# Eight weight buffers and a fourth routed group: moving work across the first table in a macaron MoE–Mamba–MoE kernel

## What is computed

```python
x = x + 0.5 * ffn(layernorm(x), router_w, w1, w2)
x = x + mamba(layernorm(x), ...)
x = x + 0.5 * ffn(layernorm(x), router_w, w1, w2)

def ffn(x, router_w, w1, w2):           # 8 experts, hidden 512, top 2
    logits = einsum('btd,ed->bte', x, router_w)
    top_vals, top_idx = top_k(logits, 2)
    top_w = softmax(top_vals)
    h = square(relu(einsum('nd,edh->enh', x, w1)))
    y = einsum('enh,ehd->end', h, w2)
    return sum over the two chosen experts of top_w * y
```

## Time and profile before

| | |
|---|---|
| median of 3 runs | 1265.07 us (1264.38 to 1267.99) |
| profiled execution | 1260.68 us, its span 1258.9 us |
| mean granted PE clock | 0.931 |
| busy in the span | PE 977.2, DVE 917.3, ACT 743.5, POOL 553.7 us |
| DMA | 154.25 MB moved, mean 123 GB/s |

### The profile page before, as it was taken

The page is one execution under the profiler, slowest core; times in us unless marked ns, Lnnn a source line. Parts: engine busy times, 40 slices in busy tenths (PEclk is TensorE's granted clock), DMA queues, the critical chain, the costliest instruction groups (busy, mean ns, idle before and its releaser), DMA issues.

```text
span 1258.9 us, 41805 instructions
## 1 busy us (share of the span) xinstructions
PE 977.2 (78%) x14928; PEld 824.7 (66%) x14928; DVE 917.3 (73%) x2840; ACT 743.5 (59%) x1751; POOL 553.7 (44%) x611
## 2 busy tenths in 40 slices
PE   1115887999938899999989999998632878899891
PEld 1115776999926677777767677776422767798791
DVE  5676665555528999999989999998866656456765
ACT  3333443566627888888878888887431543465460
POOL 5453455333332345444444444443276454433331
PEclk9998999999968999999999999999755898899996
DMA  9674444454434566666666665654324544445757
GB/s 248 211 224 102 103 108 119 103 103 96 102 101 80 108 112 119 120 116 119 120 117 119 117 119 115 123 108 89 65 77 123 103 104 107 112 110 140 181 125 234
DMA packets 205962, 154.25 MB, mean 123 GB/s; under 512 B 122752, under 2 KB 172928, under 8 KB 205632
## 3 DMA queue, kind: packets, MB, share of 16 engines
q0 software_dynamic: 41952, 72.86, 27.7%
q1 hardware_dynamic: 156896, 72.39, 24.3%
q10 hardware_dynamic: 6912, 6.32, 1.8%
HBM read 41.37 MB, written 56.10 MB: 77 GB/s over the span
## 4 chain that ended last, share of the span: by engine, by line
PE 35%; DVE 31%; issue 12%; DMA 8%; SPq 5%; ACT 4%; another core or an unknown queue 3%; POOL 2%; ACTq 1%; DVEq 0%; POOLq 0%
PE bank L773 15%; PE bank L786 13%; DVE lake L1046 7%; DVE arena L1107 3%; SPq L706 2%; DMA arena<-in_w 2%; DVE q_ L1025 2%; PE bank L1436 2%; DVE lake L1052 2%; ACT lake L1316 2%; DVE lake L1086 1%; DVE lake L1074 1%; DMA X<-yg 1%; DMA lake<-turned_y 1%
## 5 line engine op out<-in xcount | busy, mean ns | idle before, releaser
L773 PE MATMUL bank<-arena,weights 128*128 128x128 f16 x3744 | 256.1, 226 | 37.7 <-issue 30.2
L724 POOL DMA_INDIRECT ychosen<-arena,didx x156 | 157.7, 1011 | 267.5 <-issue 128.0
L773 PEld LDWEIGHTS bank<-arena,weights 128*128 x3744 | 233.7, 101 | 51.0 <-issue 47.3
L786 PE MATMUL bank<-weights,arena 128*128 x1872 | 240.9, 279 | 13.0 <-issue 9.1
L877 DVE TENSOR_TENSOR arena<-arena 128x512 f32<-128x512 f32 x156 | 107.9, 692 | 180.8 <-ACT arena L821 146.8
L821 ACT ACTIVATE arena<-bank 128x512 f32<-128x512 f32 x156 | 93.1, 597 | 212.8 <-PE bank L773 80.0
L786 PEld LDWEIGHTS bank<-weights,arena 128*128 128x128 f16 x1872 | 180.3, 100 | 39.9 <-issue 18.6
L663 POOL DMA_INDIRECT disp<-lake,sloti x128 | 132.7, 1037 | 70.2 <-issue 35.4
L1046 DVE SCALAR_TENSOR_TENSOR lake<-lake,vec 128x128 f32<-128x128 f32 x480 | 128.7, 346 | 0.0
L882 DVE TENSOR_TENSOR arena<-arena 128x512 f16<-128x512 f32 x156 | 108.1, 693 | 5.3
L1192 POOL DMA_DIRECT2D lake<-turned_y x32 | 27.9, 871 | 189.5 <-DMA turned_y<-lake 189.5
(11 more groups left out here) (176 smaller groups left out, 2010.8 us busy)
## 6 DMA issues: line engine op xcount, KB each, us to landing
arena<-in_w SPq DMA_DIRECT2D x16, 512.0 KB
yg<-ychosen SPq DMA_DIRECT2D x32, 256.0 KB, 2.8
X<-yg POOLq DMA_DIRECT2D x64, 128.0 KB, 3.6
arena<-lake SPq DMA_DIRECT2D x128, 64.0 KB, 3.3
lake<-lake POOLq DMA_DIRECT2D x32, 256.0 KB, 4.1
turned_y<-lake SPq DMA_DIRECT2D x128, 64.0 KB, 1.8
lake<-turned_y POOLq DMA_DIRECT2D x32, 256.0 KB, 4.0
lake<-ychosen SPq DMA_DIRECT2D x32, 256.0 KB, 3.7
```

Of the source, the lines that this page charges most:

```text
L724: pool.indirect_dma_start(ychosen, bass.IndirectOffsetOnAxis(ap=didx[:, t % NIDX:t % NIDX + 1], axis=0), ysb[n % YB][:, :], None).then_inc ...
L773: mm = pe.matmul(o, chunk(where, 2 * ("hl".index(w) * WN + c * HID + m * P), P), v, start=c == 0 and n_ == 0, stop=c == KD - 1 and n_ == 2)
L786: mm = pe.matmul(down_ps(n), x, chunk(where, 2 * ((2 + "hl".index(w)) * WN + c * D), D), start=c == 0 and n_ == 0, stop=c == KH - 1 and n_ ...
```

## The change

The staging ring gets eight buffers, and lies at the start of the arena, over the tiles' own buffers (`xTh`, `tails`, `hr`, `hq`, `hh`, `hl`, `ysb`). So SP's first tile load of the kernel waits for 22 used parts (the buffers under `xTh` and `tails`), and the first relu for all 32. With eight buffers the second half of x is queued after the eighth chunk, that is after all of w1. After each of the groups 0 to 3 only 4 parts (w1) are split; the 16 parts of w2 are split behind the first table. Group 4 is no longer routed before the tiles but among them; the statistics of groups 6 and 7 come right behind the first table, in one stretch, in both FFN layers. POOL sends 32 times in the tiles of a layer's first half by a new table, instead of 8 times ahead of the first store and 24 times after. The pads of the second half are all issued by ACT, one behind each of eight tiles. The spare rows of the second half are written after the first four groups. In the second FFN layer the loads and additions of finished rows and their stores begin later. The many step counters of DVE (`Chain`) become one; the waits are the same in number and place.

```diff
-NSTAGE = 3
+NSTAGE = 8
+XTH_FREE = 2 * (NSTAGE + 3)
...
-        used[0] = stage_at
+        used[0] = 0
         stage = [carve(1024) for p in range(NSTAGE)]
...
# route_dve
-                if g + 2 < NG:
+                if g + 2 < HG + 2:
                     stats(g + 2)
...
-                    for k in range(g * 8, g * 8 + 8):
+                    for k in range(g * 4, g * 4 + 4):
                         split_low(dve, k)
                 if g % HG == HG - 1:
                     yield from table(g // HG)
+                if g == HG - 1:
+                    for late in range(HG + 2, NG):
+                        stats(late)
+                    if r == 0:
+                        for k in range(2 * NCHUNK, 4 * NCHUNK):
+                            split_low(dve, k)
+                    yield ("split",)
...
# route_act
-                    for k in range(g * 8, g * 8 + 4):
+                    for k in range(g * 4, g * 4 + 2):
                         split_high(act, k)
                 if g + 1 < NG:
                     turned_rows(g + 1)
                 if r == 0 and g < HG:
-                    for k in range(g * 8 + 4, g * 8 + 8):
+                    for k in range(g * 4 + 2, g * 4 + 4):
+                        split_high(act, k)
+                if r == 0 and g == HG - 1:
+                    for k in range(2 * NCHUNK, 4 * NCHUNK):
                         split_high(act, k)
...
# route_pool
                 spare(0)
-                spare(1)
...
+                if g == HG:
+                    for late in range(HG + 2, NG):
+                        power_of(late)
+                    if r == 0:
+                        spare(1)
...
-        LATE = 14
+        LATE = 18
...
# experts_sync
                 if t == 0:
-                    pads(sp, q, range(0, E, 2))
+                    if p == 0:
+                        pads(sp, q, range(0, E, 2))
...
+                    if n == 0:
+                        sp.wait_ge(S("stage_used"), XTH_FREE)
...
-        POOL_AT = {t: ("sent", 5 + (t - 3) // (2 * GT_), (t - 3) % (2 * GT_)) for t in range(3, 3 + 3 * 2 * GT_)}
+        SEND_AT = {HG: 5, HG + 1: 11, HG + 2: 17, HG + 3: 23}
+        POOL_AT = {at + i * 7 // 8: ("sent", g, i) for g, at in SEND_AT.items() for i in range(2 * GT_)}
...
-        PE_AT = {0: ("turned", 5), 2: ("logits", 5), 5: ("ranks", 5), 6: ("turned", 6), 8: ("logits", 6), 12: ("ranks", 6),
-                 13: ("turned", 7), 15: ("logits", 7), 19: ("ranks", 7)}
+        PE_AT = {3: ("ranks", 4), 4: ("turned", 5), 6: ("logits", 5), 9: ("ranks", 5), 10: ("turned", 6), 12: ("logits", 6),
+                 15: ("ranks", 6), 16: ("turned", 7), 18: ("logits", 7), 21: ("ranks", 7)}
...
-                    pe.wait_ge(S("stage_used"), 4 * NCHUNK)
+                    pe.wait_ge(S("stage_used"), 2 * NCHUNK)
...
-        ACT_AT = {0: ("turned", 5), 2: ("rows", 6), 4: ("ratio", 5), 6: ("turned", 6), 9: ("rows", 7), 11: ("ratio", 6),
-                  13: ("turned", 7), 18: ("ratio", 7)}
-        PADS_AT = 24
+        ACT_AT = {1: ("rows", 5), 2: ("ratio", 4), 5: ("turned", 5), 7: ("rows", 6), 8: ("ratio", 5), 11: ("turned", 6),
+                  13: ("rows", 7), 14: ("ratio", 6), 17: ("turned", 7), 20: ("ratio", 7)}
+        PADS_AT = 25
...
# relu
+                if n == 0:
+                    act.wait_ge(S("stage_used"), 4 * NCHUNK)
...
-                if s == PADS_AT:
-                    pads(act, 2 * r + 1, range(1, E, 2))
-                if r and s >= TILES + LATE + 8 and (s - TILES - LATE - 8) % 5 == 0 and (s - TILES - LATE - 8) // 5 < 4:
-                    store_rows(act, (s - TILES - LATE - 8) // 5)
+                if PADS_AT <= s < PADS_AT + E:
+                    pads(act, 2 * r + 1, [s - PADS_AT])
+                late = s - TILES - LATE - 5
+                if r and 0 <= late < HT and late % 4 == 0:
+                    store_rows(act, late // 4)
...
-        DVE_AT = {0: ("stats", 7), 1: ("norm", 6), 3: ("choose", 5), 4: ("low", 6), 5: ("place", 5), 8: ("norm", 7),
-                  10: ("choose", 6), 11: ("low", 7), 12: ("place", 6), 17: ("choose", 7), 19: ("place", 7),
-                  20: ("table", 1, 0), 21: ("table", 1, 1), 22: ("table", 1, 2), 23: None}
+        DVE_AT = {0: ("norm", 5), 1: ("choose", 4), 2: ("low", 5), 4: ("place", 4), 6: ("norm", 6), 7: ("choose", 5),
+                  8: ("low", 6), 10: ("place", 5), 12: ("norm", 7), 13: ("choose", 6), 14: ("low", 7), 16: ("place", 6),
+                  19: ("choose", 7), 22: ("place", 7), 23: ("table", 1, 0), 24: ("table", 1, 1), 25: ("table", 1, 2), 26: None}
...
-            until(routing, ("place", HG))
+            until(routing, ("split",))
...
-                if r and TILES + LATE - 4 <= s < TILES + LATE - 4 + HT:
-                    combine(dve, s - (TILES + LATE - 4))
+                if r and TILES + LATE - 2 <= s < TILES + LATE - 2 + HT:
+                    combine(dve, s - (TILES + LATE - 2))
```

150 lines of the change are left out of this document (60 added, 90 removed).

## The result

The changed kernel takes 1254.13 us (median of 5 runs, 1250.32 to 1259.26), the kernel before 1265.07 on the same chip: a ratio of 0.990 (95% interval 0.9876 to 0.9924). It is faster by 10.9 us, not by the forecast 31.4, and 1254 lies outside the range of 1221 to 1250. The profiled execution took 1259.26 us (span 1257.5).

The account below looks back on a forecast made before the run. Bounds: SP's ring waiting for DVE's splits before 103 us, sends beside first-half tiles, then PE's own pace. Gains 24.9 (start) + 0 (group 4) + 5 + 1.5 (last half) = 31.4 from 1265.1 give 1234 us, range 1221 to 1250.

Parts of the forecast that it names:

- The start: Start of the first FFN layer: first relu at 80.8 instead of 105.7 us, 24.9 us gained.
- the group pace: Routing before the tiles: DVE takes 11.2 us a group, POOL's 11.9 sets the pace; group 3's sends begin at 60.1.
- the pads: Before the first tile load: four pads take 4.5 us of issue, the load begins 4.3 later, at about 73.
- just fit: DMA budget before the first tile load: 17.2 MB, moved by 62 us at 239, then 297 GB/s.
- the lock between DVE and POOL: Splits beside group sends: by the skill's rule the start gains 17.5 instead of 24.9; judged much less, as rival 0.05.
- Group 4 among the tiles: First-half tiles of both layers: moving group 4's routing there costs 0, range -8 to +8 us for each layer.
- Rival D: First-half tiles: first tiles run free of sends, later ones absorb them; -8 us in each layer, 1218 us; chance 0.12.
- what holds PE: First-half tiles: 32 sends beside them cost PE 1.26 us each, 40.4 us lost, and stay 32 after the change.
- The second layer's start: Second FFN layer's first matmul: it follows the last send's landing, not group 4, so moving that group brings 0.
- The last half: Last half's tiles: later loads and additions gain 5 us (0 to 9.8), the earlier last store of rows 1.5.
- under 8: Last half, a sign that the prediction is right: DVE's waits for block loads stay under 8 us.
- rival A: Start worth less: first groups at 13 us each and DMA late, start gains 9, 1249.6 us; chance 0.13.

Follow-up runs that it names:

- ring3: Changed kernel with three staging buffers, eight splits after each group and none behind the table: ratio 0.9954 to the kernel before, first relu at 105.0 us.
- mamba_late_third: Changed kernel with SP's loads of the Mamba weights moved behind its first eight tile loads: median 1170.73 us, first relu at 84.3 us.
- after_third: The changed kernel, unchanged, run again on the faster kind of chip: median 1170.15 us, first relu at 89.0 us.
- extra_sends: Changed kernel with group 5's eight sends repeated in each layer into a tensor nobody reads: 20.0 us more than the changed kernel, on the chip of 1264 us.
- before_third: The kernel before, unchanged, run again on the faster kind of chip: 1192.86 us, first relu at 105.3 us.
- set 1: One of five sets of runs, each on one chip; the kernel before takes 1195.57 us in it.
- g4_ahead: Changed kernel with group 4 routed ahead of the tiles again, and the tables, early sends and pads of the kernel before: ratio 0.9806 to the kernel before.
- late14: Changed kernel with the second layer's block loads, additions and stores of finished rows back at their earlier places: ratio 0.9804 to the kernel before.
- set 2: One of five sets of runs, each on one chip; the kernel before takes 1263.39 us in it.
- set 4: One of five sets of runs, each on one chip; the kernel before takes 1192.86 us in it.
- mamba_late_again: Changed kernel with the Mamba weights loaded behind the first eight tile loads, in another set: 0.28% faster than with one send a tile, first relu at 84.8 us.

## Why the prediction was wrong, step by step

**The start: right mechanism, term mis-sized, 15 instead of 24.9.** DVE no longer waits behind the ring, and all of the gain comes from it (`ring3`). The working of the group pace fits a chip of 1195 us: sends of group 3 begin at 58.41 (forecast 60.1), and the splits end at 80.4 in `mamba_late_third` (forecast 79.1). The step that failed is the pads: "SP issues the loads of the Mamba weights, then its pads", charged with 4.5 us of issue and 4.3 to the load. The loads themselves were left out twice. Their issue stands ahead of the pads, and their bytes (three of 512 KB, and 128, 82.5 and 64 KB, 1.8 MB together) are missing from the 17.2 MB that "just fit". The 4.5 and the 4.3 come from a kernel that had the same six loads ahead of its pads, but there 3.0 us lay between them (the last load ended at 87.16, the pads began at 90.18); now it is 1.1 us (69.12 and 70.25). A second thing was put at nothing without a reason: the seven spare stores of the second half, 0.9 MB that the change moves to this place. The budget has only the seven of the first half. The profile after, SP, ACT and POOL from 62 to 90 us:

```profile
62.45 1.13 POOL L656 DMA_INDIRECT disp<-lake,sloti  x1 [2.03 <-DVE sloti L410]
63.88 1.45 POOL L656 DMA_INDIRECT disp<-lake,sloti  x1 [0.30 <-issue]
65.64 0.97 POOL L656 DMA_INDIRECT disp<-lake,sloti  x1 [0.30 <-issue]
...
67.57 0.81 SPq L948 DMA_DIRECT2D wo<-in_wo  x1
...
70.25 6.28 SPq L665 DMA_DIRECT2D disp<-zrow  x4
...
71.29 4.18 ACTq L665 DMA_DIRECT2D disp<-zrow  x4
...
74.95 9.71 DVE L317 SCALAR_TENSOR_TENSOR weights<-arena,weights 128x512 f16<-128x512 f32 x16
...
82.85 1.32 SPq L702 DMA_TRANSPOSE arena<-disp  x1
```

and the chain that ended last, at the same place (start, length, what):

```profile
70.25 1.63 SPq L665
...
76.19 6.55 DMA disp<-zrow
82.85 1.32 SPq L702
```

The pads are issued until 76.5 instead of 68.7, and land 6.3 later instead of 4.3: the load starts at 82.85 where the prediction had 74. With the Mamba weights moved it is 74.59, but the first relu comes 3.1 us earlier and not 8, because then the tile's own load lands some 3 us late beside the spare stores and PE starts 6.9 us behind it, not 4.0. The chip of 1264 us adds another delay: the sends of group 3 begin at 62.45 there instead of 58.41, and the first relu is at 90.0 and 91.2 there for 87.3 on the mean of the other kind, 3 us. How the 9.2 us by which the first relu misses the forecast divide stays open: 3.1 go with the loads, some 3 with the spare stores where they meet the first tile, 3 with the kind of chip, and the three overlap.

The prediction also weighed the lock between DVE and POOL (the Trainium skill, SBUF — State Buffer, "Reading the diagram"). The second row above is a send beside the splits, 1.45 us, the third the usual one, 0.97; in `after_third` the first two sends of the same group, beside the splits, take 1.09 and 1.03. So beside the splits POOL loses at most 0.6 us a group (1.13 and 1.45 for twice 0.97), not four whole splits (2.46). The trace doesn't bear the rule out for these sends, and its 17.5 comes near the measured gain of 15.2 by luck.

**Group 4 among the tiles: the step that failed, 0 forecast.** In the profiles tiles 0 to 39 take 151.1 and 153.3 us (150.7 and 152.2 again) for 143.7 and 142.3 (141.8 and 147.2): 8.1 a layer on the means. The medians have room for half of it: 15.2 at the start and 3.3 in tiles 52 to 77 are 18.5, the gain is 10.9, and that leaves 7.6 for both layers. So the loss is 4 to 8 us a layer, between the 0 that was taken and the "+8" end. Profiled executions don't tell which. The count of the sends was taken as the cost ("they are 32 after the change too"). In rows of the source line of the send, tiles 8 to 32 of the first layer, before and after (count, duration, first and last start):

```profile
L663 POOL DMA_INDIRECT disp<-lake,sloti x21: 970/974/1475, 144.5 to 222.9; - x21
```

```profile
L656 POOL DMA_INDIRECT disp<-lake,sloti x31: 968/972/1456, 114.9 to 218.6; - x31
```

Ten more sends stand in this stretch, and it loses 44.4 us against PE's own pace instead of 26.4: 1.43 a send instead of 1.26. Of the 32 sends before, one to four came ahead of a layer's first relu and cost the tiles nothing, and the first eight tiles now lose 2.7 us without a single send. So the loss can be told as three parts: sends that had been free, a higher price of each, and first tiles that didn't become fully free. That is a division of one sum, not three measured causes: `extra_sends` has 1.25 for a further send, and why a send of the new table costs more than one of the old is open. Rival D (the first tiles run free and the others absorb the sends) had the first half right and the second wrong.

What the loss is made of shows in the waits, here of the changed kernel from 114 to 222 us on the chip of 1264 us (who waited for what, us in all, times, longest):

```profile
POOL ychosen L720 <- issue: 45.6, 25, 4.0
ACT arena L818 <- remote: 41.5, 8, 8.2
DVE arena L872 <- ACT arena L818: 35.1, 13, 7.4
...
PE bank L769 <- issue: 18.8, 30, 1.4
```

and of the same program from 112 to 208 us on a chip of 1195 us:

```profile
ACT arena L818 <- PE bank L769: 19.2, 19, 1.8
DVE arena L872 <- ACT arena L818: 18.0, 15, 3.2
POOL ychosen L720 <- issue: 13.3, 30, 2.4
...
PE bank L769 <- issue: 0.4, 2, 0.2
```

`issue` is a wait for nothing that the profile shows. PE stands so 30 times; here it does so inside a tile's 24 matmuls, where no semaphore is waited for:

```profile
146.13 0.22 PE L769 MATMUL bank<-arena,weights 128*128 128x128 f16 x1 [0.97 <-issue]
...
146.93 0.27 PE L769 MATMUL bank<-arena,weights 128*128 128x128 f16 x2 [0.58 <-issue]
...
148.41 0.27 PE L769 MATMUL bank<-arena,weights 128*128 128x128 f16 x1 [1.21 <-issue]
...
149.13 0.27 PE L769 MATMUL bank<-arena,weights 128*128 128x128 f16 x1 [0.45 <-issue]
```

Matmuls come one or two at a time, 0.7 to 1.5 us apart, and the granted clock is lower with them; whether it adds to the loss or only follows the gaps is not shown. These two rows are the changed kernel from 113 to 222 us on the one kind of chip and from 112 to 208 on the other:

```profile
113.00:222.00 109.00, 84.96 (x984) 73.43 (x982) 57.37 (x190) 42.70 (x86) 56.30 (x56) 0.89 0.44 107
```

```profile
112.00:208.00 96.00, 94.22 (x1323) 88.56 (x1320) 71.59 (x220) 58.92 (x114) 68.99 (x66) 1.00 0.65 150
```

So the prediction's "what holds PE" comes with these sends on chips of the one kind, and it is absent on the other. There POOL is the bound, as the upper end of the term had it: sends and stores follow each other without a gap, at 3.0 us a tile, and 24 x 3.0 = 72 is what 8 to 32 takes in the profiles there with the new table of sends (71.4 to 72.9 in six executions, two layers each). Before, with fewer sends in the stretch, it was 68.0. What delays PE's instructions on the one kind is not settled. The Trainium skill (Runtime: NRT & Kernel Launch, "Instruction fetch mechanics") says that engines fetch instructions in blocks of 16 KiB by DMA, mostly hidden. The profile agrees with the size of the blocks (125 packets, 2.05 MB on the instruction queue, on both kinds of chip). Whether the gaps are such a fetch made late by the sends, no run here shows. The trace speaks against it in the rows above: from 142.6 to 151.2 us the two instruction queues moved nothing, and PE went on behind its gaps without a new block.

**The second layer's start, 0: right.** The last send lands at 957.72 (the chain, start and length), and the first matmul follows 3.8 us behind it, as before (966.96 and 970.73):

```profile
954.67 3.05 DMA disp<-lake,sloti
...
961.53 2.74 PE L769 MATMUL bank<-arena,weights 128*128 128x128 f16 x24 [15.15 <-DMA arena<-disp]
```

From the last relu of the first layer to the first of the second it is 623.1 and 624.2 us, for 625.0 and 622.5.

**The last half, 5 + 1.5: 3.3 measured.** DVE's wait for block loads is the term that moved, 1144 to 1230 us of both:

```profile
DVE X L915 <- DMA lake<-ychosen: 14.2, 11, 2.8
```

```profile
DVE X L910 <- DMA lake<-ychosen: 7.9, 4, 3.4
```

That is the "under 8" of the prediction. But the interval gain is 3.3 (77.35 to 74.05 on the means of two), and nothing came at the very end: from the last relu to the end it is 30.1 and 29.9 us for 29.4 and 29.5, so the 1.5 for the last store was not there.

**The sum.** On the chip of 1264 us, medians: 15 at the start, 3.3 in tiles 52 to 77, 7.6 lost in the stretches, 10.9 in all. Of the 20.5 us between this and the forecast, 9.7 are the start, 7.6 the stretches and 3.2 the last half. On the other kind, spans of `before_third` and `after_third`: 16.3 at the start, 3.2 in 52 to 77, 1.8 and 1.5 lost in the stretches, and 24.6 in all. The other 8.5 of those lie in stretches that the change doesn't touch (4.1 of them in tiles 39 to 52 of the second layer), in one execution of each. In number the outcome is nearest to rival A joined with the upper end of the stretch term; A's own reason, groups of 13 us each, is not what happened. The list gave A 0.13 alone and had no case for both.

## What to carry to other kernels

Before a wait is declared to set a start, list everything that the same queue issues ahead of it and add its bytes to the budget: here six loads, put there for the layer after, cost 3 us in front of four pads, and seven stores that only the second half needs came in the way of the first tile. When work is moved from a place where nothing waits to one where something does, its unit price must be taken from the place that it moves to, not as a mean over both. And when a stretch loses time to waits for nothing that the profile shows, profile the same program in several sets, on other chips and at another time, before giving that loss to the kernel: 22 to 26 us of the 26 to 31 lost in tiles 8 to 32 before the change are absent from `before_third`.

The lowest medians are those with the Mamba weights behind the eighth tile load: 1167.65 in set 1, where `g4_ahead` has 1171.75 and `late14` 1173.08, and with group 4 ahead of the tiles 1249.05 against 1253.53 in set 2. None of these differences is clear of the intervals, and in set 4 there is none.

## What the runs showed of the hardware

- One program takes 1263 to 1265 us in two sets and 1193 to 1197 us in four. Nearly all of the difference of some 70 us is in the two stretches with indirect sends beside matmuls (tiles 0 to 39: 143.7 against 110.1 us), while the first layer's stretch without sends agrees within some 2 us (tiles 39 to 77: 100.7 against 102.8 in `before_third`, 100.7 in most others). Sets 2 and 3, on different levels, carry the same chip number, so this need not be a lasting trait of a chip.
- On the slower kind each further indirect send beside the tiles costs 1.25 us, more than its own 0.97 us on POOL and about the 1.28 from one send to the next. The DMA share is 0.44 there and 0.65 on the other kind, so DMA is the less busy one where the sends cost more.
- DVE's `rk` of group 1 starts 2.8 us after the last rank matmul (31.52 to 34.30) on the slower kind, with 1.99 us of its wait put down to no engine ("remote"). On the faster kind it is 0.7 (32.26 to 32.97). PE's word comes late there as well, before any tile runs.
- Four pads of 129.5 KB take 4.4 us of issue on SP where no loads of the Mamba weights stand ahead, 4.5 and 4.7 us where those 1.8 MB were issued up to 3.0 us before them (the kernel before), and 6.3 us where they were issued up to 1.1 us before them (the changed kernel).
- The second part of a tile's load lands 1.8 to 1.9 us after its issue in the kernel before, and 4.7 to 5.0 us after it while seven stores of 129.5 KB from POOL's queue are in flight (`ring3`, `mamba_late_again`, `mamba_late_third`).
